# The maximum pass of a fused perceiver kernel: chunks taken in pairs as b + relu(a - b), all of it through four PSUM bank pairs in one order

## The reference, cut to what matters

```python
q = (query @ Wq + bq)            # 128 x 256, 16 heads of 16
k = (key_value @ Wk + bk)        # 12544 x 256
attn = jnp.einsum('bhqd,bhkd->bhqk', q, k) * scale
attn = jnp.clip(attn, -CLAMP, CLAMP)
attn = jax.nn.softmax(attn, axis=-1)
```

## Time and profile before

| | |
|---|---|
| median of the runs | 1149.45 us |
| the profiled execution | 1144.78 us, its span 1142.9 us |
| PE busy | 944.5 us (83%) |
| DVE busy | 645.1 us (56%) |
| ACT busy | 537.1 us (47%) |
| mean granted TensorE clock | 0.927 |
| maximum pass | about 29 to 251 us of the span |

### The profile page before, as it was taken

One profiled execution on the slowest core, in us unless ns is written; L12 is line 12 of the kernel. 1 busy time (PEld: TensorE's weight loads), 2 busy tenths in 40 slices (PEclk: granted clock), 3 DMA queues, 4 the chain that ended last, 5 costly groups with the idle time before them and its releaser, 6 DMA issues.

```text
span 1142.9 us, 21211 instructions
## 1 busy us (share of the span) xinstructions
PE 944.5 (83%) x7651; PEld 699.5 (61%) x7651; DVE 645.1 (56%) x936; ACT 537.1 (47%) x626; POOL 173.4 (15%) x93
## 2 busy tenths in 40 slices
PE   3878888758999999999988758885999989999414
PEld 2545555536777777777756546554887868887303
DVE  5778999872111122222252144994878767778592
ACT  2787888627666666666645512100333323333011
POOL 4000000131111111111175022133003030000000
PEclk9988999779999999999998769998999999999765
DMA  7213121154565665555634332112001000000000
GB/s 211 74 42 122 48 71 57 32 129 87 130 140 130 144 145 128 128 128 128 143 82 98 112 102 56 29 50 55 1 1 38 1 6 1 1 1 1 1 0 5
DMA packets 37319, 81.73 MB, mean 72 GB/s; under 512 B 9553, under 2 KB 17426, under 8 KB 37138
## 3 DMA queue, kind: packets, MB, share of 16 engines
q1 hardware_dynamic: 37266, 81.01, 28.5%
HBM read 41.54 MB, written 0.13 MB: 36 GB/s over the span
## 4 chain that ended last, share of the span: by engine, by line
PE 44%; issue 20%; DVE 11%; SPq 9%; ACT 8%; DMA 6%; POOL 1%; DVEq 1%; ACTq 0%; POOLq 0%
PE ps L1498 9%; SPq L310 8%; DMA ks<-khl 6%; PE ps L1291 5%; PE ps L1508 5%; PE ps L1519 4%; PE ps L1303 4%; PE ps L1245 4%; PE ps L1273 4%; PE ps L1500 2%; DVE cm L813 1%; ACT pr L555 1%; ACT oacc L555 1%; PE ps L1282 1%; ACT khl L592 1%
## 5 line engine op out<-in xcount | busy, mean ns | idle before, releaser
L617 ACT ACTIVATE pr<-ps 128x1024 f32<-128x1024 f32 x196 | 199.9, 1026 | 131.6 <-DVEq L966 128.2
L1291 PE MATMUL ps<-qs,ks 128*128 128x256 f32 x784 | 146.4, 309 | 23.2 <-DMA ks<-khl 14.6
L1245 PE MATMUL ps<-ks 128*128 128x448 f32 x448 | 135.2, 424 | 32.3 <-ACT pr L555 13.5
L1291 PEld LDWEIGHTS ps<-qs,ks 128*128 128x128 f32 x784 | 106.0, 190 | 66.3 <-issue 38.1
L1498 PE MATMUL ps<-ks,ct 128*128 128x512 f32 x448 | 126.1, 404 | 6.9 <-issue 4.2
L813 DVE TENSOR_REDUCE cm<-ps 128x1 f32<-128x896 f32 x112 | 120.7, 1085 | 16.1 <-PE ps L1245 14.7
L1245 PEld LDWEIGHTS ps<-ks 128*128 128x128 f32 x448 | 80.8, 206 | 75.4 <-DVE cm L813 25.1
L1303 PE MATMUL ps<-pr,v 128*17 128x128 f32 x3136 | 125.3, 278 | 0.2 <-ACT pr L617 0.2
L847 DVE SCALAR_TENSOR_TENSOR khl<-ps,bk,khl 128x448 fp32r<-128x448 f32 x56 | 38.2, 683 | 151.5 <-ACT khl L592 151.5
L695 ACT ACTIVATE pr<-ps 128x1024 f32<-128x1024 f32 x56 | 57.6, 1029 | 110.5 <-DVE ps L1096 109.7
L405 POOL TENSOR_TENSOR ct<-raw,ct 128x896 fp32r<-128x896 f32 x14 | 30.6, 2188 | 498.5 <-ACT ct L537 498.5
(11 more groups left out here) (260 smaller groups left out, 1307.4 us busy)
## 6 DMA issues: line engine op xcount, KB each, us to landing
ks<-khl SPq DMA_DIRECT2D x168, 224.0 KB, 4.8
raw<-in_ctxT SPq DMA_DIRECT2D x36, 448.0 KB, 3.8
raw<-in_ctxT SPq DMA_DIRECT2D x54, 224.0 KB, 4.3
ffw<-in_mask_q SPq DMA_DIRECT2D x1, 1568.0 KB, 9.3
ffw<-in_W1T SPq DMA_DIRECT2D x1, 1024.0 KB, 4.9
ffw<-in_W2T SPq DMA_DIRECT2D x1, 1024.0 KB, 7.3
pr<-in_Wq SPq DMA_DIRECT2D x1, 1024.0 KB, 5.0
pr<-in_Wkt SPq DMA_DIRECT2D x1, 1024.0 KB, 7.3
```

The source lines that it names most:

```text
L617: nc.scalar.activation(pr[:, (HALVES * b + u) % 4, :], bank(2 * (u % 2), 2), ACT.Exp).then_inc(S["e0_exp"], 1)
L1245: last = mm(ps[:, bank + n, 0:NB], qn[:, h, :], kn[:, b, t, n * NB:(n + 1) * NB], start=True, stop=True)
L1291: last = mm(ps[:, 2 * z + k // 2, (k % 2) * 256:(k % 2) * 256 + 256], ks_v[:, b, gg, t * P:(t + 1) * P], qs[:, gg * 256:gg * 256 + 256], s ...
```

## The change

Two chunks form a pair, a the second and b the first. For each head, max over both is max(b + relu(a - b)). The keys of b and the differences of the keys (a minus b) are kept in `kn`, so that one matmul unit ("above") gives a - b and another ("base") gives b. ACT takes relu of the above unit into one of four float32 buffers (`stage`). DVE adds the base unit from PSUM and takes the maximum over the row in one instruction (`tensor_tensor_reduce`, the form that the layer 1 pass already has at L1062). There are seven pairs, 32 units in each. `acc`, its fill on GpSimd, its fold at the end, the bf16 stages and L813 and L819 go away.

All units go through the four bank pairs in turn: above 0, base 0, above 1, base 1, and so on, with the next pair's key projections as units of their own after heads 2 and 5 (keys of b) and after heads 8 and 11 (keys of a). A unit waits for the reader of the unit four places earlier. ACT reads the projected keys of b after its relu of heads 3 and 6; DVE forms the differences after heads 9 and 12. ACT splits the next two chunks after heads 8 and 14 of each pair, and the first four chunks before the first relu. In the last pair the sum pass's first keys and values are such units too, and they are read after heads 2, 5 (keys) and 8, 10, 12, 14 (values).

The mask is no longer summed on ACT; DVE takes the maximum of each group's 448 int32 words, one after each of heads 4 to 10 of the first pair, and SP's `ffw` loads wait for those. The memset of 32 partitions of `ks` on GpSimd is divided in two, since the second key buffer lies in its first part.

The core of the diff:

```diff
-HEAD_BANKS = (0, 2, 6)
+def pair_order(extra):
+    order = []
+    for h in range(H):
+        order += [("above", h), ("base", h)] + extra.get(h, [])
+    return order
+FULL = pair_order({2: [("keys", 0)], 5: [("keys", 1)], 8: [("diff", 0)], 11: [("diff", 1)]})
+LAST = pair_order({1: [("key0", 0)], 4: [("key0", 1)], 7: [("value0", 0)], 9: [("value0", 1)],
+                   11: [("value0", 2)], 13: [("value0", 3)]})
+def unit_bank(order, kind, i):
+    return 2 * (order.index((kind, i)) % 4)
...
 # ScalarE
-            split_max0(0, 0)
-            for i in range(4):
-                key_block_max0(0, 0, i)
-            split_max0(1, 1)
+            def above_base(s, h):
+                at = unit_bank(FULL if s < NSUP - 1 else LAST, "above", h)
+                act.wait_ge(S["m0_head"], UNITS * s + 2 * h + 1 + UNITS)
+                act.wait_ge(S["m0_red"], H * s + h - SLOTS + 1 + H)
+                nc.scalar.activation(stage[:, h % SLOTS], ps[:, at:at + 2, 0:NB], ACT.Relu
+                                     ).then_inc(S["m0_staged"], 1)
+            split_max0(0, 0)
+            for t in range(2):
+                base_keys(0, t)
+            split_max0(1, 1)
+            split_max0(2, 0)
+            split_max0(3, 1)
+            for s in range(NSUP - 1):
+                for h in range(H):
+                    above_base(s, h)
+                    if h in (3, 6):
+                        base_keys(s + 1, (3, 6).index(h))
+                    if h == 8:
+                        if s < NSUP - 2:
+                            split_max0(2 * s + 4, 0)
...
+                    if h == 14 and s < NSUP - 2:
+                        split_max0(2 * s + 5, 1)
...
 # VectorE
+            def head_max(s, h, order=FULL):
+                at = unit_bank(order, "base", h)
+                dve.wait_ge(S["m0_head"], UNITS * s + 2 * h + 2 + UNITS)
+                dve.wait_ge(S["m0_staged"], H * s + h + 1 + H)
+                V.memset(pause2[:, h % 2:h % 2 + 1], 0.0)
+                nc.vector.tensor_tensor_reduce(
+                    out=stage[:, h % SLOTS], in0=ps[:, at:at + 2, 0:NB], in1=stage[:, h % SLOTS],
+                    scale=1.0, scalar=-3.0e38, op0=ALU.add, op1=ALU.max,
+                    accum_out=cm[:, h:h + 1]).then_inc(S["m0_red"], 1)
+            def pair_max0(s, buf, masks=False):
+                dve.wait_ge(S["m0_merge"], s + 1)
+                for h in range(H):
+                    head_max(s, h)
+                    if h in (9, 12):
+                        t = (9, 12).index(h)
+                        key_differences(s + 1, t, 1 - buf, unit_bank(FULL, "diff", t))
+                    if masks and 4 <= h < 4 + NSUP:
+                        any_kept(h - 4)
+                merge_max0(s)
...
 # TensorE
+            def slot_free(order, s, q):
+                if s is None or q >= 4:
+                    kind, i = order[q - 4]
+                    back = 0
+                else:
+                    kind, i = FULL[len(FULL) + q - 4]
+                    back = -1
+                if kind == "above":
+                    pe.wait_ge(S["m0_staged"], H * (s + back) + i + 1 + H)
+                elif kind == "base":
+                    pe.wait_ge(S["m0_red"], H * (s + back) + i + 1 + H)
+                elif kind == "keys":
+                    pe.wait_ge(S["m0_keys"], 2 * (s + 1 + back) + i + 1)
+                elif kind == "diff":
+                    pe.wait_ge(S["m0_diff"], 2 * (s + 1 + back) + i + 1 + 2)
...
```

More of the change, by code:

```diff
@@ L844, in key_block_lo @@
+            for t in range(2):
+                key_differences(0, t, 0, 4 + 2 * t)
+            pair_max0(0, 0, masks=True)
+            with dve.Fori(1, NSUP - 2, 2) as s:
+                for e in range(2):
+                    pair_max0(s + e, 1 - e)
+            pair_max0(NSUP - 2, 1)
             def key_block_lo(c, i):
@@ new lines, in project_max0 @@
+            def project_max0(s, e, t, at):
+                if t == 0:
+                    pe.wait_ge(S["m0_split"], 2 * s + e + 1)
+                for n in range(2):
+                    dst = ps[:, at + n, 0:NB]
+                    mm(dst, wk0[:, W_AH, t * P:(t + 1) * P], ct[:, e, X_AH, n * NB:(n + 1) * NB],
+                       start=True, stop=False)
+                    last = mm(dst, wk0[0:64, W_BH, t * P:(t + 1) * P], ct[0:64, e, X_B, n * NB:(n + 1) * NB],
+                              start=False, stop=True)
+                last.then_inc(S["m0_proj"], 1)
@@ new lines, in head_scores @@
+            def head_scores(s, buf, kind, h, at):
+                t = h // 8
+                if h % 8 == 0 and kind == "above":
+                    pe.wait_ge(S["m0_keys"], 2 * s + t + 1)
+                    pe.wait_ge(S["m0_diff"], 2 * s + t + 3)
+                for n in range(2):
+                    last = mm(ps[:, at + n, 0:NB], qn[:, h, :],
+                              kn[buf][:, 1 if kind == "above" else 0, t, n * NB:(n + 1) * NB],
+                              start=True, stop=True)
+                last.then_inc(S["m0_head"], 1)
@@ L1265, in project0, with pair_max0 @@
-            def project0(c, b, i):
+            for e in range(2):
+                for t in range(2):
+                    if e == 1:
+                        pe.wait_ge(S["m0_keys"], t + 1)
+                    project_max0(0, e, t, 4 + 2 * t)
+            def pair_max0(s, buf, first=False):
+                for q, (kind, i) in enumerate(FULL):
+                    if first and q < 4:
+                        if q >= 2:
+                            pe.wait_ge(S["m0_diff"], q - 2 + 1 + 2)
+                    else:
+                        slot_free(FULL, s, q)
+                    at = unit_bank(FULL, kind, i)
+                    if kind in ("above", "base"):
+                        head_scores(s, buf, kind, i, at)
+                    else:
+                        project_max0(s + 1, 0 if kind == "keys" else 1, i, at)
@@ L1267, in project0 @@
+            pair_max0(0, 0, first=True)
+            with pe.Fori(1, NSUP - 2, 2) as s:
+                for e in range(2):
+                    pair_max0(s + e, 1 - e)
+            pair_max0(NSUP - 2, 1)
+            def project0(c, b, i, at=5, emptied=1):
                 t, n = i // 2, i % 2
@@ L1277, in values0 @@
             def values0(c, b, t, bank=7, emptied=1):
[L1280 removed]
+                if emptied:
+                    pe.wait_ge(S["e0_v"], TPC * c + t + emptied)
                 for j, (w, xx) in enumerate(PAIRS):
```

283 lines of the change are left out of this document (100 added, 183 removed).

## The result

The changed kernel takes 1184.55 us (median of 4 runs, 1181.37 to 1191.47) against 1150.09 (4 runs of the kernel before on the same chip): ratio 1.0308, 95% interval 1.026 to 1.0356. It is slower by 34.4 us; 1184 had been forecast, with 1160 to 1214 as the range. The profiled execution is the longest of the four (1191.47, span 1189.6, granted clock 0.901; the others 0.912 to 0.920).

A forecast was written before the change was run, and what follows sets the result against it. Waits in the ring's order, not engine work (about 20.5 us), were taken to bound a pair at 30.5. 46.2 + 4 x 30.5 + 33.8 + 29.1 + 37.2 = 268.4, plus 18 for clock, gave 1184 us; range 1160 to 1214.

The forecast's parts named there:

- The ring, legs 1 to 5: Chain of waits through one pair's 16 heads, in five parts of 5.6, 5.3, 6.8, 6.6 and 6.2 us: 30.5 together.
- the splits (legs 3 and 5): Heads 7 to 10 and 13 to pair end: ACT's 1.69 us splits lie on the chain; parts of 6.8 and 6.2 us.
- the differences (3 and 4): Heads 7 to 13: base 10 and 13 wait for DVE's 1.15 us key differences; parts of 6.8 and 6.6 us.
- the key copies (1 and 2): Heads 0 to 7: base 4 and 7 wait for ACT's 1.01 us key copies; parts of 5.6 and 5.3 us.
- The start: DVE's first pass over a head at 46.2 us, 16.9 later, behind ACT's splits and the fourth chunk's load.
- The end: What stands before and behind the maximum pass was taken as unchanged, so nothing was added after its last merge.
- The clock: PE standing still about 2.5 us twice a pair, before base 10 and 13, lowers its clock: 18 us over the pass.
- The sum: Pass end at 268.4 us at full clock, 286 with clock loss, 35 later; profiled execution 1180, median 4.7 above: 1184.
- The mask sums: Mask sums leave ACT (12.0 us) and SP's weight loads stop waiting; the saving is inside the comparison of pass ends.
- The ring that overlaps: Rival: ACT runs ahead, a pair costs 20.5 us, total 1097; below 28.0 a pair the late start is repaid; chance 0.12.
- The clock that stays up: Rival: gaps of 2.5 us do not lower PE's clock; total 1167; chance 0.17.
- the clock mostly down: Rival: gaps and smaller waits keep PE's clock low in every pair; about 1207, at most 1227; chance 0.12.

The follow-up runs named there:

- the key copies' pair: A pair of the changed kernel with only ACT's two key copies one head earlier (after relus 2 and 5): 1181.06 us, ratio 1.0273.
- the readers earlier: The changed kernel with key copies after relus 2 and 5 and key differences after passes 8 and 11, each one head earlier: 1144.61 us, ratio 0.9969.
- the new order: The changed kernel with projections and their readers re-placed, start changed, weight sums inside the sixth pair, GpSimd's memset and split out of DVE's way: 1101.56 us, ratio 0.9589.
- masks and start set right: The kernel before with mask maxima on DVE ahead of the first head, accumulator fill behind DVE's first operations, first transpose's copy ahead of weight casts: 1125.74 us.

## Why the prediction was right, and where it was not

**The ring, legs 1 to 5: right.** 30.5 us a pair at the full clock; 30.76 and 31.06 measured where the clock is 1.00, 31.34 at 0.95. The waits are where the legs put them: base 4 behind the key copy, the pass over 9 behind a relu behind the split, base 10 and 13 behind the differences, the pass over 10 starting 0.93 us after the difference (0.8 said). The experiments touch the legs apart: the splits (legs 3 and 5) and the differences (3 and 4) moved the time by at least what their legs say, the key copies (1 and 2) by half. The first pair, counted at 30.5, took 33.74 where the granted clock reads 1.00 (the kernel with GpSimd's split out of the way). Of the 3.0 us that this is above the pair behind it, 2.0 had come together by the pass over 3, ahead of the mask maxima (the projection's matmuls take up to 0.74 there, for 0.47 later), and 1.0 since: the maxima cost little, but not nothing.

**The start: 3.4 us too late** (46.2 against 42.79). The step took the third chunk's load at 37.25 as fixed, "nothing in the change hastens it". GpSimd's memset of `ks`, cut from 7680 to 4096 columns, had held the normalisation on DVE, and with it the query rows ahead of that load in SP's queue. From that load on the step holds: the first pass begins 2.8 us behind the start of the fourth chunk's split, 2.7 forecast.

**The end: 5.5 us missed.** "What stands before and behind it is not changed" was wrong: GpSimd's split falls beside the merge (3.2 us, shown), and the transposes take 6.33 for 5.21 us, at a granted clock of 0.54 in that stretch where before it was 0.69.

**The clock: 18 us assumed, too much.** Without it the sum ran from 46.2 to 268.4 (its own terms give 268.3), 222.2 us; the profiled execution took 246.6, 24.4 more. Some 4.4 of that stand in pairs at full clock too (3.2 in the first, 0.3 in each of the next three, 0.4 in the fifth), and if the 6.9 us by which this execution is above the median are clock as well, some 13 are left for a median run. Keeping PE busy in the two named gaps returned 7; with it the last two pairs still ran at granted clocks of 0.87 and 0.83. The mechanism was half right: both gaps are there (2.45 and 2.38 us for some 2.5), but the lower level does not follow from them alone. The fourth and fifth pair of this execution have them at granted clocks of 0.95 and 0.99, and the key copies' pair at 1.00.

**The sum.** The spans differ by 46.7. The execution shown of after is 6.9 above its median, the one of before 5.3 below (1144.78 against 1150.09), which leaves 34.5, the measured 34.4. I had expected the profiled one of after 4.7 below its median, as before. So the 1184 rests on one main term that held, the ring, and on misses of both signs beside it, in a median run: start -3.4, clock -5, pairs +4.4, end +5.5, the rest of the program +2.9, and the profiled execution of before -5.3. That they cancel to less than 1 us is luck; that the kernel is slower by some tens of us, and by this chain, is not.

**The mask sums.** That they would be "inside the comparison" held, but it hides the account: the mask part alone is 15.5 us faster, so the ring of units, in this order, costs 50, not 34.

**The rivals.** The ring that overlaps (0.12, 20.5 us a pair, break-even 28.0) is refuted for this order, and for another borne out in its direction, though no pair came down to 20.5: with the readers earlier (25.7 to 26.6) it comes level with the kernel before and just passes it, though not the kernel before with the mask part alone (1144.6 against 1134.2). With the new order (23.65) it is 2.1% faster than the kernel before with masks and start set right, and 4% than the kernel before as it was. The break-even of 28.0 was set too high: 26.4 us a pair gave 1151.65, since the 5 us at the end were not in it, nor the first pair's 30.0. The Trainium skill (Perfetto Trace Analysis, Matmuls) would have matmul groups rotate through PSUM banks so that evacuation overlaps. Here they rotate, and PE stands 2.45 us ahead of one; in a ring the rule holds only where every slot's reader is prompt. Its other rule (Optimizing Scalar/DVE Operations), to break long instructions up, was not tried. The clock that stays up gave 1177 with PE kept busy, and not 1167; the clock mostly down did not come.

**Left open.** Why the clock stays up in some pairs and falls in others that have the same two gaps, and how its loss divides over the smaller gaps; no run here separates them.

## What to carry to other kernels

In a ring of buffers with several readers, write for each slot what its reader has ahead of it in its own queue: two late places in the order of one engine cost 33 us here, and no sum of busy times shows it. Put every reader directly behind the reader of the unit that stands ahead of its own, as the two fastest orders of the ring here do, and take a ring's price from the chain of one period before building it. Where a change gains and loses, time its parts apart: the mask part was worth 15.5 us by itself and lay hidden under a loss of 50. The same holds for a win: of the 46 us of the last kernel 22 are not the ring's.

## What the runs showed of the hardware

Some of VectorE's instructions stood still beside GpSimd's: 6.73, 3.74 and 3.68 us for 128 x 256 beside memsets of 6.49, 3.51 and 3.51 (0.41 without), and 1.65 and 1.93 for 16 columns beside 2.07 and 2.09 (0.17 without). The wait lasted until GpSimd's own instruction ended. The Trainium skill (GPSIMD Engine Reference, Specifications) names the shared interface to SBUF and contention with VectorE's two-port modes and two SBUF inputs; the cases above agree with it and show the price. Others were not held. In the sixth pair of the changed kernel GpSimd works beside a pass over a head and a key difference, each with one operand in PSUM, and they take what they take elsewhere:

```profile
229.15 2.09 POOL L405 TENSOR_TENSOR ct<-raw,ct 128x896 fp32r<-128x896 f32 x1 [221.07 <-issue]
...
230.00 1.09 DVE L815 CUSTOM_DVE_ANT_0 pr<-ps,pr 128x896 f32<-128x896 f32 x1
...
231.02 1.15 DVE L804 SCALAR_TENSOR_TENSOR ks<-ps,bk,ks 128x896 fp32r<-128x896 f32 x1
```

And the merge, two operands in SBUF, took 0.17 us beside a memset, where beside GpSimd's TENSOR_TENSOR it took 1.65; so the skill's row covers more than these runs bear out:

```profile
245.50 3.09 POOL L415 MEMSET ks<- 32x3584 f32 x1 [12.09 <-PE ps L1260]
...
247.22 0.17 DVE L823 TENSOR_TENSOR mx<-mx,cm 128x16 f32<-128x16 f32 x1
```

GpSimd is held too: in the kernel before, its split beside the fold takes 3.30 and 2.80 us, not 2.07 and 2.09.

TensorE's level does not follow from the length of one gap. Pairs with the same two gaps, or one a little shorter (1.7 to 2.5 us), ran at granted clocks of 0.80, 0.95, 0.99 and 1.00; one with a gap of 4.1 and one of 1.7 at 0.71 (0.66 in the neighbours); and pairs two to five at 0.94 to 1.00 where the gaps were filled or gone. I had taken the gap as the price of a late reader; where the lower level came behind it, it was up to as much again: some 4 us of a pair against 3.4 with the longer splits.
